# Low parts of the expert weights on GpSimd instead of VectorE

## What is computed

```
probs = softmax(t @ gate_w);  topw, topi = top_k(probs, 2);  topw = topw / sum(topw)
up    = einsum('th,ehf->etf', t, w1)                 # 8 experts, h = 256, f = 1024
gated = relu(up) * einsum('th,ehf->etf', t, w3)
down  = einsum('etf,efh->eth', gated, w2)
out   = einsum('eth,te->th', down, combine)          # combine holds the two shares per token
```

## Time and profile before

| | |
|---|---|
| three unprofiled executions | 1099.15, 1101.43, 1103.42 us |
| median | 1101.43 us |
| the profiled execution | 1103.58 us |
| its span in the trace | 1101.8 us |
| mean granted TensorE clock | 0.945 of full speed |
| busy share of the span: PE, DVE, ACT, POOL | 88%, 73%, 68%, 40% |

### The profile page before, as it was taken

How to read it: one execution, slowest core, us unless ns; L and a number is a source line. 1 busy time by engine, 2 the same in 40 slices (tenths; PEclk the granted TensorE clock), 3 DMA queues, 4 the chain that set the end, 5 groups by cost and what they waited for, 6 DMA issues and landing times.

```text
span 1101.8 us, 22969 instructions
## 1 busy us (share of the span) xinstructions
PE 972.7 (88%) x6862; PEld 907.3 (82%) x6862; DVE 801.7 (73%) x2330; ACT 750.2 (68%) x2119; POOL 435.5 (40%) x520
## 2 busy tenths in 40 slices
PE   4759999999889899999999999999993699999982
PEld 2549888998789799988999999999982599999971
DVE  6739989889889677777776776777756466666646
ACT  2248778888788688788787788787864155555530
POOL 2346657868555443432353232222227610000033
PEclk8869999999999899999999999999995699999996
DMA  8669798896455686466556454545103655555223
GB/s 181 155 157 269 214 219 227 226 241 173 115 148 151 167 193 161 120 163 137 140 144 139 125 162 108 163 122 136 22 2 117 206 160 164 147 161 160 70 66 103
DMA packets 146574, 166.18 MB, mean 151 GB/s; under 512 B 79555, under 2 KB 101315, under 8 KB 141331
## 3 DMA queue, kind: packets, MB, share of 16 engines
q1 hardware_dynamic: 129427, 143.27, 50.2%
q0 software_dynamic: 3536, 10.82, 3.2%
q10 hardware_dynamic: 13488, 10.63, 3.1%
HBM read 105.88 MB, written 58.79 MB: 149 GB/s over the span
## 4 chain that ended last, share of the span: by engine, by line
PE 58%; DVE 16%; ACT 10%; issue 9%; DMA 2%; another core or an unknown queue 2%; POOL 1%; SPq 1%; ACTq 1%; DVEq 0%; POOLq 0%
PE psO L1026 14%; PE psS L993 10%; PE psX L1003 8%; PE psY L1042 6%; PE psP L925 6%; ACT wgt_hi L1261 4%; DVE pbuf L1678 3%; PE psS L1181 2%; PE psX L1181 2%; DVE gated L2000 2%; PE psO L1009 2%; DVE pTl L1700 2%; PE psP L955 2%; PE psP L938 1%
## 5 line engine op out<-in xcount | busy, mean ns | idle before, releaser
L1293 ACT ACTIVATE pbuf<-pbuf,nmax 128x256 f32<-128x256 f32 (+3 forms) x512 | 263.9, 517 | 40.0 <-DVE nmax L1678 39.1
L993 PE MATMUL psS<-kT,qE 128*128 128x256 f32 (+3 forms) x1024 | 238.7, 318 | 25.5 <-DVE nmax L1678 23.8
L1678 DVE CUSTOM_DVE_ANT_0 pbuf<-psS,mcau 128x256 f32<-128x256 f32 (+3 forms) x512 | 219.7, 434 | 50.0 <-PE psS L993 44.5
L1700 DVE TENSOR_TENSOR pTl<-psX,pTh 128x512 fp32r<-128x512 f32 x272 | 186.8, 687 | 72.2 <-ACT pTh L1261 71.4
L1261 ACT ACTIVATE pTh<-psX 128x512 fp32r<-128x512 f32 x272 | 160.4, 590 | 57.9 <-PE psO L1026 40.3
L993 PEld LDWEIGHTS psS<-kT,qE 128*128 128x128 f32 x1024 | 161.5, 194 | 38.0 <-DVE nmax L1678 31.8
L1026 PE MATMUL psO<-pTh,vpad 128*128 128x256 f32 x1088 | 187.3, 294 | 4.9 <-DVE oS L1706 3.5
L765 POOL TENSOR_TENSOR ol<-oS,oh 128x256 fp32r<-128x256 f32 x128 | 94.9, 741 | 200.8 <-ACT oh L1261 196.3
L1003 PE MATMUL psX<-idn,pbuf 128*128 128x128 f32 x1088 | 163.6, 276 | 8.0 <-ACT pbuf L1293 6.8
L1026 PEld LDWEIGHTS psO<-pTh,vpad 128*128 128x128 f32 x1088 | 150.1, 190 | 13.4 <-DVE oS L1706 6.9
L1003 PEld LDWEIGHTS psX<-idn,pbuf 128*128 128x128 f32 x1088 | 127.7, 142 | 14.6 <-ACT pbuf L1293 7.0
(11 more groups left out here) (278 smaller groups left out, 2337.1 us busy)
## 6 DMA issues: line engine op xcount, KB each, us to landing
qd<-st SPq DMA_DIRECT2D x32, 1024.0 KB, 4.4
qE<-qd SPq DMA_DIRECT2D x128, 256.0 KB, 5.9
mrawV<-in_w_moe SPq DMA_DIRECT2D x32, 384.0 KB
mrawB<-in_w_moe SPq DMA_DIRECT2D x32, 384.0 KB
kT<-kd SPq DMA_DIRECT2D x64, 128.0 KB, 4.1
kT<-kd SPq DMA_DIRECT2D x32, 256.0 KB, 4.2
kd<-st SPq DMA_DIRECT2D x7, 1024.0 KB, 4.8
xg<-sq ACTq DMA_DIRECT2D x7, 640.0 KB, 4.9
```

Of the source, the lines that this page charges most:

```text
L993: last = mm(psS[j % 2][:, 0:n], qE[:, g % 2, j, t * P:(t + 1) * P], kT[:, g % 2, c, k0:k0 + n], start=(c == 0), stop=(c == 1))
L1293: nc.scalar.activation(pj, pj, ACT.Exp, bias=nmax[:, u % 4, j:j + 1], scale=-1.0, accum_out=sums[:, u % 4, j:j + 1]).then_inc(a_exp, 1)
L1678: V.tensor_tensor_reduce(probs(u, j), psS[j % 2][:, 0:n], mcau[:, SEQ - n:], -SCALE, 3e38, ALU.add, ALU.min, nmax[:, u % 4, j:j + 1]).then ...
L1700: V.tensor_tensor(pTl[:, kt % 2, :], psX[kt % 2][:, :], pTh[:, kt % 2, :], ALU.subtract).then_inc(v_pl, 1)
```

## The change

GpSimd makes all low parts of the weights of experts 1 to 7. In `results` it makes pieces 0 to 6 between the stores of the output and the load of tokens, and piece 7 after that load. Before its loops it waits until all 8 low pieces of expert 0 are counted. VectorE's two calls of `split_lo` in the pass are gone.

```diff
+            def low_pieces(e, i, pieces):
+                for q in pieces:
+                    pool.wait_ge(w_hi, NPC * i + NPC + q + 1)
+                    apart(pool)
+                    at = slice(q * PC, (q + 1) * PC)
+                    G.tensor_tensor(wgt_lo[(e + 1) % 2][:, at], raw_piece(q), wgt_hi[(e + 1) % 2][:, at], ALU.subtract)\
+                     .then_inc(w_lo, 1)
...
                 pool.dma_start(yg[bass.ds(i * TP + 2 * P, TP - 2 * P), :], ysb[XT * P - TP:P, 2, :]).then_inc(st_y, 16)
+                low_pieces(e, i, range(NPC - 1))
                 tokens(e, i, j)
+                low_pieces(e, i, range(NPC - 1, NPC))
...
             pool.dma_start(xin[:, :, :], xg[TP:TP + XT * P, :].rearrange("(j p) d -> p j d", p=P)).then_inc(ld_xg, 16)
+            pool.wait_ge(w_lo, NPC)
             experts(pool, lambda e, first: apart(pool), results, range(NE - 1))
...
                     if f == 0:
                         store(i, begun[0], j) if e == NE - 1 else store(i)
-                    if e + 1 < NE and f < NF - 1:
-                        split_lo(e + 1, f, NPC * i + NPC)
                 tokens_lo(i + 1)
-                if e + 1 < NE:
-                    split_lo(e + 1, NPC - 1, NPC * i + NPC)
```

## The result

The changed kernel took 1126.45 us (median of 4, 1125.32 to 1130.97) against 1102.4 us for the kernel before (median of 4): ratio 1.0221, 95% interval 1.0199 to 1.0243. It is 24 us slower, where 4 us less had been forecast and the range ended at 1105.5. The profiled execution took 1130.97 us with a span of 1129.2, 27.4 us over the span of before.

The account below looks back on a forecast made before the run. TensorE was taken as the bound. Boundary gain -4.9, gTl stalls +4.0 and clock -3.1 summed to -4.0 us: 1099.6 from the profiled 1103.58, or 1097.4 against the median 1101.43; range 1092.5 to 1105.5.

Parts of the forecast that it names:

- The gain at the boundary: End of a pass: without VectorE's subtraction, slice 7's gated, gTl and down come sooner; 0.7 us a pass, 4.9 in seven.
- Costs put at nothing: GpSimd's added pieces delay token loads, raw-weight loads, TensorE's piece waits and the wait before the loops at no cost.
- rival "nobody blocks": In the pass, gTl slips in or hand-over is faster, stall under 0.2 us: -8.2 us, 1093.2 us; chance 0.18.
- That `gTl` pays, once a pass, and why GpSimd is late: gTl reads two SBUF operands, so GpSimd's pieces block it; one stall a pass; stores make GpSimd begin 1.6 us late.
- It gets through at 910.83 and ends 0.38 us later: Pass 1, slice 2: gTl, asking at 909.27, enters as piece 1 ends and finishes at 911.2; its down was due 910.53.
- got through as each piece ended: Token routing: a VectorE operation on two SBUF tensors entered at each piece's end, some 0.12 us after the next's recorded start.
- The term of 0.7 us a pass: TensorE's stall before slice 2's down, 0.7 us (bounds 0 and 0.95) in six passes: 4.2 us lost, less 0.2.
- Piece 0 starts behind it at 907.3: Pass 1: gTl of slice 1 runs 906.80 to 907.29, ahead of GpSimd's piece 0, which starts at 907.3.
- a small gain: Pass 0: GpSimd's stores stand later against the slices, no stall comes and a short TensorE wait goes, 0.2 us.
- The clock: Two clock falls at pass boundaries, 1.55 us each, go as the gap shrinks: 3.1 us gained (bounds 0 and 3.1).
- The slower rival: GpSimd falls out of step in the slices, its pieces turning round too slowly: +6 us, 1107.4 us; chance 0.12.

Follow-up runs that it names:

- the version with one operand in PSUM: The changed kernel, with the subtraction making gTl reading psTr (PSUM) in place of gated in slices 1 to 6, low part left out there: 1094.36 us, ratio 0.9924.
- with the memset: The changed kernel with output stores moved behind pieces 0 to 6 and a waited-for GpSimd memset of 1280 columns in their old place: 1108.64 us (one execution).
- with pauses: The changed kernel, but each GpSimd piece also waits until the piece before it is counted as done: 1106.6 us, ratio 1.0026.
- the memset and its wait: The changed kernel with a GpSimd memset of 8 columns between the two stores and piece 0, and a wait for its completion: 1100.32 us, ratio 0.997.

## Why the prediction was wrong

**The gain at the boundary: right.** 0.7 us a pass was forecast. Passes without a block take 23.87 us in place of 24.5, 0.64 us. The gap before the last `down`, 1.02 us in the earlier trace rows, is 0.31 us, where 0.3 was forecast.

**Costs put at nothing: right.** Tokens, raw loads, the wait before the loops and the counts cost nothing in the version with one operand in PSUM: 1094.4 us, against the 1093.2 of the rival "nobody blocks".

**That `gTl` pays, once a pass, and why GpSimd is late: right.** It is two SBUF operands beside a GpSimd that reads SBUF, one long-held `gTl` a pass, where GpSimd starts its pieces late behind its stores. The Trainium skill, page "SBUF — State Buffer", section "Who interferes with whom", speaks of one instruction that excludes the other until it is done. The runs agree where no run of pieces stands directly behind a store: a hold of 1.4 us (1.90 less 0.49, with the memset) to 1.9 us (2.40 less 0.49, with pauses), at most one piece. They differ behind a store, where the hold lasts for two to four pieces. They differ too on who goes first: by the page it is whoever issues second that blocks, and in passes 2 to 6 the held `gTl` is the one recorded first (a recorded start need not be the issue).

**The step that failed** is "It gets through at 910.83 and ends 0.38 us later", with the sentence it rested on, that VectorE "got through as each piece ended". Those rows are pieces with no transfer just before them. In the loop the pieces stand right behind two stores of GpSimd, and there a waiting VectorE is passed over at every end of a piece until GpSimd runs dry. Pass 1 shows this step by itself: `gTl` of slice 2 asked about 0.1 us after piece 1 had begun, nearly as forecast, and came through not at that piece's end but at the next one's. The term of 0.7 us a pass was 3.12 us (2.64 in pass 1). The 0.38 us from the last piece's end was right (0.37).

**A second step failed before it:** "Piece 0 starts behind it at 907.3". I had `gTl` of slice 1 go ahead of piece 0 because it asks first. In passes 2 to 6 it is recorded 0.19 to 0.21 us ahead of piece 0, while the second store is under way, and is held all the same. So the held one was that of slice 1, not of slice 2, in six of the seven passes. With pauses between the pieces, where only one piece holds it, TensorE waits 1.36 us; I estimate from it that this step alone would have cost about that, in place of 0.7. Pass 0, for which I counted a small gain, had a wait of 3.76 us, and 0.93 us even with the memset and its wait. Its stores do stand later against the slices, but the held `gTl` was not clear of them.

**The clock.** The two falls of the earlier trace rows went in seven of the eight versions without long blocks: their granted clock from 895 to 1050 us is 1.00, against 0.98 before. The eighth, with the stores behind the pieces, is at 0.98 and has its two falls. I had judged falls in mid-pass unlikely on the strength of a 0.7 us stall, and with waits of 0.86 and 1.36 us a pass none came between 895 and 1050 us. At 2.64 to 3.76 us they came in five of the six passes from 1 to 6 and in pass 0, for 7 us more in passes 1 to 6.

**The slower rival** had the sign and not the mechanism: pieces are paced by their high parts, and one started 0.15 us behind its high part (896.69 to 896.83 us in pass 0, 931.55 to 931.70 with piece 0 on VectorE), so the handover added nothing that the forecast lacked.

With the memset and its wait the kernel has the forecast's gain and clock and nearly its stall: passes of 24.7 us, 23.87 + 0.86, and a ratio of 0.997 where the forecast amounts to 0.9963 (1097.4 / 1101.43).

## What to carry to other kernels

Before moving work to GpSimd, list what VectorE runs beside it with two SBUF operands, and count the wait for a whole GpSimd operation for each that is on the critical path. Don't let GpSimd run several operations directly behind a transfer that it issues: complete one small operation first, or leave the first piece to another engine. And move only the pieces whose place is on the path: three of eight gave 5.8 us of a gain of 8.0.

## What the runs showed that I had not expected

- A run of GpSimd operations right behind a transfer issued by GpSimd holds VectorE's two-operand instruction to the end of the run: 5.5 us for three pieces and 7.35 to 7.75 for four, against 2.0 us without the transfer. Why is open. The length of four pieces doesn't tell: they take 7.07 us with VectorE kept out, and also 7.07 when it is let in with 64 columns (7.32 with 320). Nor was the same run tried with the stores issued by another engine.
- A completed memset of 8 columns undoes it; the same memset without the wait does not.
- With GpSimd's stores at the end of the pass, TensorE's gap between two experts grew from 0.8 us to between 1.4 and 1.6 us, in both versions that have them there; the cause is open.
